# Top-128 search in a four-layer transformer kernel: the last count moves to VectorE, and TensorE builds two lists in PSUM for MAX8

## The reference, cut to what matters

```python
draft = einsum('bhqd,bhkd->bhqk', qr, kr) + causal_mask
_, draft_indices = top_k(draft, 128)             # num_remain = 128 for S = 512
mask = full(neg); mask[..., draft_indices] = 0.0 # then causal again
scores = einsum('bhqd,bhkd->bhqk', qr, kr) / sqrt(16) + mask
attn = softmax(scores); out = (attn @ v) @ Wo.T
```

## Time and profile before

| | |
|---|---|
| median of 3 runs | 2380.08 us (2378.83 to 2393.21) |
| profiled execution | 2377.4 us, its span 2375.6 us |
| mean granted TensorE clock | 0.834 |
| busy: PE / DVE / ACT / POOL | 1707.7 / 1615.9 / 1293.2 / 1017.7 us |

### The profile page before, as it was taken

The page is one execution under the profiler, slowest core; times in us unless marked ns, Lnnn a source line. Parts: engine busy times, 40 slices in busy tenths (PEclk is TensorE's granted clock), DMA queues, the critical chain, the costliest instruction groups (busy, mean ns, idle before and its releaser), DMA issues. The chain is left out here.

```text
span 2375.6 us, 25955 instructions
## 1 busy us (share of the span) xinstructions
PE 1707.7 (72%) x7274; PEld 1270.8 (53%) x7274; DVE 1615.9 (68%) x3711; ACT 1293.2 (54%) x3343; POOL 1017.7 (43%) x699
## 2 busy tenths in 40 slices
PE   5899998999898699998655433652545553387997
PEld 4777777777777578876422222331322222245885
DVE  3777777777776545656338898879779888822435
ACT  3555656556555332334167878776787778252221
POOL 3445545545444256552012344545434434632442
PEclk9999999999999799998556667775767776687998
DMA  4112111111111122212300000200000000001111
GB/s 151 32 43 91 41 50 56 67 57 54 60 41 58 54 80 104 82 53 99 58 7 7 7 8 1 27 7 1 8 7 7 7 7 1 1 0 45 48 45 49
DMA packets 33570, 96.40 MB, mean 41 GB/s; under 512 B 4048, under 2 KB 16720, under 8 KB 29264
## 3 DMA queue, kind: packets, MB, share of 16 engines
q1 hardware_dynamic: 33456, 95.20, 12.2%
HBM read 87.84 MB, written 7.34 MB: 40 GB/s over the span
## 5 line engine op out<-in xcount | busy, mean ns | idle before, releaser
L198 PE MATMUL PS<-XT,AR 128*128 128x512 f32 x2472 | 617.6, 405 | 26.0 <-POOL AR L805 12.3
L198 PE MATMUL PS<-AR 128*128 128x512 f32 (+2 forms) x2568 | 552.2, 370 | 100.4 <-issue 69.8
L198 PEld LDWEIGHTS PS<-AR 128*128 128x128 f32 x2568 | 449.5, 195 | 196.3 <-issue 91.5
L198 PEld LDWEIGHTS PS<-XT,AR 128*128 128x128 f32 x2472 | 469.4, 192 | 138.4 <-issue 16.8
L1244 POOL TENSOR_TENSOR AF<-AF 128x512 f32<-128x512 f32 (+3 forms) x64 | 148.5, 2320 | 487.7 <-DVE AF L1449 487.7
L1185 ACT ACTIVATE AF<-PS 128x512 f32<-128x512 f32 x160 | 94.0, 594 | 255.8 <-PE PS L1065 134.5
L1052 PE MATMUL PS<-AR,XT 48*128 48x128 f32 (+3 forms) x256 | 127.5, 498 | 142.4 <-DVE BF L1312 74.7
L1080 PE MATMUL PS<-AF,BF 128*128 128x512 f32 x320 | 191.6, 703 | 20.7 <-ACT AF L1185 20.5
L1100 PE MATMUL PS<-BF,AF 128*128 128x1 f32 x24 | 7.0, 362 | 264.3 <-DVE BF L1410 264.3
L559 POOL TENSOR_TENSOR AF<-AF 128x512 f32<-128x512 f32 (+1 forms) x64 | 107.6, 1681 | 167.8 <-DVE AF L690 167.8
L553 POOL TENSOR_TENSOR AF<-AF 128x512 f32<-128x512 f32 x80 | 103.3, 1292 | 168.2 <-ACT AF L345 168.2
(11 more groups left out here) (171 smaller groups left out, 3616.0 us busy)
## 6 DMA issues: line engine op xcount, KB each, us to landing
AF<-in_mean_w SPq DMA_DIRECT2D x48, 448.0 KB, 3.3
AF<-in_ffn_w SPq DMA_DIRECT2D x14, 1536.0 KB, 6.5
AF<-in_attn_w SPq DMA_DIRECT2D x9, 1536.0 KB, 6.4
AF<-in_attn_w SPq DMA_DIRECT2D x9, 1024.0 KB, 5.0
AF<-in_ffn_w SPq DMA_DIRECT2D x11, 769.0 KB, 4.4
XT<-rope_scratch SPq DMA_DIRECT2D x96, 64.0 KB, 2.7
rope_scratch<-BF SPq DMA_DIRECT2D x20, 256.0 KB, 2.3
AF<-in_x SPq DMA_DIRECT2D x8, 256.0 KB, 3.8
```

Of the source, the lines that this page charges most:

```text
L198: last = nc.tensor.matmul(dst, lhs(a, c), rhs(m, c), start=(first and k == 0), stop=(k == 3 * n - 1 and not more))
```

## The change

- The fourth count leaves ScalarE. VectorE does it with `mark`: 0 where a key is at or above the threshold, -1 where not, written as bf16 into one of three row buffers, and summed on the way.
- TensorE makes two lists for each head in PSUM (`lists`), by adding large numbers to recomputed scores: one where only keys below the threshold keep their score, one with negated scores where only keys above keep it. `pick` is now one MAX8 on each, straight from PSUM. The negated keys lie at partitions 64 to 111 (GpSimd, `negate`), so key and query tiles are loaded twice, at partitions 0 and 64.
- The aim is now 128, with up to 7 keys missing or too many. `cut` looks in both lists.
- The four score banks become one ring of slots for scores and lists (`ring_full`, `ring_free`).
- TensorE's loop begins with the 16 `lists` of x - 1. SyncE waits for `keys_read(x - 2)`.
- ScalarE's order is count 0, exp 0, count 1, exp 1, count 2, then the copies and exp 2 and 3. Update 2 on VectorE moves behind `evac` of q = 2.

```diff
-AIM = TOPK - (WINDOW + 1) // 2
+SIDE = (WINDOW + 1) // 2
+AIM = TOPK
...
+        def scored(x, h):
+            return 16 * x + 32 * before(x - 1) + h
+        def listed(x, h, side):
+            return 16 * min(x + 2, NB) + 32 * before(x) + 2 * h + side
+        def keys_read(x):
+            return (listed(x, 15, 1) if tile_of(x)[1] > 0 else scored(x, 15)) + 1
...
-                for x in (2 * n, 2 * n + 1):
-                    if x >= 2:
-                        sp.wait_ge(A1["scores"], 16 * (x - 1))
+                if x >= 2:
+                    sp.wait_ge(A1["ring_full"], keys_read(x - 2))
                 if n % QT == 0:
-                    if b > 0:
-                        sp.wait_ge(A1["scores"], QT * 32)
-                    for a, s in enumerate((0, 1, 0)):
-                        src = scr[b, 4, s].rearrange("(c h) t -> c h t", c=HD1)
-                        sp.dma_start(f32(kst[a * HD1:(a + 1) * HD1]), src).then_inc(A1["kst"], 16)
+                    for low in (0, 64):
+                        for a, s in enumerate((0, 1, 0)):
+                            src = scr[b, 4, s].rearrange("(c h) t -> c h t", c=HD1)
+                            sp.dma_start(f32(kst[low + a * HD1:low + (a + 1) * HD1, 4 * hf:4 * hf + 4]),
+                                         src[:, 4 * hf:4 * hf + 4]).then_inc(A1[f"kst{hf}"], 16)
+                for low in (0, 64):
                     for j in range(2):
                         for a, s in enumerate((0, 0, 1)):
...
+            def slot(k):
+                wait(pe, A1["ring_free"], k - 3)
+                return PS[:, k % 4]
...
+            def lists(x, h):
+                n, i, hf, W = tile_of(x)
+                q, k = qst[:, x % 2, h, :], kst[:, 4 * hf + h // G1, 0:W]
+                mark = above[:, h % 3, 0:W]
+                pe.wait_ge(A1["above"], 16 * before(x) + h + 1)
+                dst = slot(listed(x, h, 0))
+                nc.tensor.matmul(dst[:, 0:W], ident_b, causal_big[:, SEQ - W:SEQ], start=True, stop=False)
+                nc.tensor.matmul(dst[:, 0:W], negbig_b, mark, start=False, stop=False)
+                nc.tensor.matmul(dst[:, 0:W], q[0:48], k[0:48], start=False, stop=True).then_inc(A1["ring_full"], 1)
+                if h % 8 == 0:
+                    pe.wait_ge(A1["kneg"], 2 * (n // QT) + hf + 1)
+                dst = slot(listed(x, h, 1))
+                nc.tensor.matmul(dst[:, 0:W], big_b, mark, start=True, stop=False)
+                nc.tensor.matmul(dst[:, 0:W], q[64:112], k[64:112], start=False, stop=True).then_inc(A1["ring_full"], 1)
...
             for x in range(-1, NB + 2):
                 xp = x - 1
+                if 0 <= xp < NB and tile_of(xp)[1] > 0:
+                    for h in range(16):
+                        lists(xp, h)
                 if x + 1 < NB:
                     scores(x + 1, 0)
...
+            def mark(x, h):
+                n, i, hf, W = tile_of(x)
+                if h == 0:
+                    dve.wait_ge(A1["thr"], ROUNDS * (before(x) + 1))
+                v.tensor_scalar(above[:, h % 3, 0:W], S1[x % 2][:, h, 0:W], st["thr"][:, h:h + 1], -1.0,
+                                ALU.is_ge, ALU.add, accum_out=acc[:, 2, h:h + 1]).then_inc(A1["above"], 1)
+            def pick(x, h):
+                W = tile_of(x)[3]
+                for side in range(2):
+                    k = listed(x, h, side)
+                    dve.wait_ge(A1["ring_full"], k + 1)
+                    v.max(best[:, h, SIDE * side:SIDE * side + SIDE], PS[:, k % 4, 0:W]).then_inc(A1["ring_free"], 1)
...
             def cut(x):
+                step(v.tensor_scalar(missing, acc[:, 2], -1.0, float(TOPK - W), ALU.mult, ALU.add))
+                step(v.tensor_tensor(hit, at_tau.unsqueeze(1).to_broadcast([P, 16, 16]), rows, ALU.is_equal))
+                dve.wait_ge(A1["ring_free"], listed(x, 15, 1) + 1)
+                step(v.tensor_tensor(val, hit, best, ALU.mult))
+                step(v.tensor_reduce(below, val[:, :, 0:SIDE], AX.X, ALU.add))
+                step(v.tensor_reduce(over, val[:, :, SIDE:2 * SIDE], AX.X, ALU.add))
+                step(v.tensor_tensor(st["tau"][:, x % 2], below, over, ALU.subtract))
+                step(v.tensor_tensor(gap[:, :, 0:WINDOW], best[:, :, 0:WINDOW], best[:, :, 1:WINDOW + 1], ALU.is_gt))
+                step(v.tensor_tensor(hit, at_gap.unsqueeze(1).to_broadcast([P, 16, 16]), rows, ALU.is_equal))
+                step(v.tensor_tensor(val, hit, gap, ALU.mult))
+                v.tensor_reduce(flag_row, val.rearrange("p h s -> p (h s)"), AX.X, ALU.add).then_inc(A1["cut"], 1)
...
-                for pair in range(8):
+                if topk:
+                    mark(xp, 0)
+                    mark(xp, 1)
+                for h in range(16):
                     if topk:
-                        pick(xp, pair)
-                    if search and pair in (2, 5):
-                        update(x, (pair - 2) // 3)
-                    if done >= 0 and pair == 3:
+                        if h + 2 < 16:
+                            mark(xp, h + 2)
+                        pick(xp, h)
+                    if search and h in (6, 14):
+                        update(x, (h - 6) // 8)
+                    if done >= 0 and h == 7:
...
-                    if done >= 0 and pair == 7:
+                    if done >= 0 and h == 15:
                         dve.wait_ge(A1["yproj"], done + 1)
...
                     if x + 1 < NB:
                         evac(x + 1, q)
+                    if search and q == 2:
+                        update(x, 2)
...
+    at_tau = np.concatenate([np.where(j < SIDE - 1, j + 1, NONE), -j])
```

More of the change, by code:

```diff
@@ L957, in build_kernel @@
         A1 = names("a1", "raw_qkv", "raw_wo", "wq_hi", "wq_lo", "wk_hi", "wk_lo", "wv_hi", "wv_lo", "wo_hi", "wo_lo",
[L958 to L959 removed]
+                   "tables", "vproj", "v", "vz", "stored0", "stored1", "kst0", "kst1", "qst0", "qst1", "mask", "mask_r",
+                   "ring_full", "ring_free", "kneg", "above", "tiny", "stat", "nmax", "thr", "acc", "cut", "tau",
                    "flag_ps", "exp", "final", "rinv", "pnorm", "turned", "pt", "pv", "o_hi", "o_lo", "yproj", "yadd")
@@ L1046, in scores @@
                 if q == 0:
[L1047 to L1052, removed]
-                                     start=True, stop=False)
-                    nc.tensor.matmul(PS[:, h, W - P:W], ident_r, mask_r, start=False, stop=True)\
-                        .then_inc(A1["scores"], 1)
+                    pe.wait_ge(A1[f"kst{hf}"], 96 * (n // QT + 1))
+                    pe.wait_ge(A1[f"qst{x % 2}"], 16 * 12 * (x // 2 + 1))
+                for h in range(4 * q, 4 * q + 4):
+                    dst = slot(scored(x, h))
+                    nc.tensor.matmul(dst[:, 0:W], qst[0:48, x % 2, h, :], kst[0:48, 4 * hf + h // G1, 0:W],
+                                     start=True, stop=False)
+                    nc.tensor.matmul(dst[:, W - P:W], ident_r, mask_r, start=False, stop=True)\
+                        .then_inc(A1["ring_full"], 1)
+            def lists(x, h):
[12 more added lines that the diff above has]
+                nc.tensor.matmul(dst[:, 0:W], q[64:112], k[64:112], start=False, stop=True).then_inc(A1["ring_full"], 1)
             def values(x, q):
@@ L1188, in act_attn1 @@
                 xp = x - 1
-                search = x < NB and tile_of(x)[1] > 0
-                counted = 0
-                def last_round(heads=1):
-                    nonlocal counted
-                    if search:
-                        upto = min(counted + heads, 16)
-                        count(x, ROUNDS - 1, range(counted, upto))
-                        counted = upto
+                search, shown = x < NB and tile_of(x)[1] > 0, 0 <= xp < NB
                 if search:
@@ L1407, in cut @@
-                step(v.tensor_tensor(val, hit, best[:, :, 1:WINDOW + 1], ALU.mult))
-                step(v.tensor_reduce(after, val, AX.X, ALU.add))
-                step(v.tensor_tensor(after, after, st["tau"][:, x % 2], ALU.is_lt))
-                v.tensor_reduce(flag_row, after, AX.X, ALU.add).then_inc(A1["cut"], 1)
+                missing, below, over = st["square"], st["err"], st["scaled"]
+                rows = missing.unsqueeze(2).to_broadcast([P, 16, 16])
+                dve.wait_ge(A1["above"], 16 * (before(x) + 1))
@@ L1471, in dve_attn1 @@
                     cut(xp)
-                if search:
-                    update(x, 2)
                 if 0 <= xp < NB and xp % (2 * QT) == 0:
```

184 lines of the change are left out of this document (80 added, 104 removed).

## The result

| | before | after |
|---|---|---|
| median | 2381.39 us (2378.83 to 2393.21, 4 runs) | 7710.32 us (7695.58 to 7712.71, 4 runs) |
| profiled span | 2375.6 us | 7708.3 us |
| granted TensorE clock, mean | 0.834 | 0.613 |

The change makes the kernel 3.233 times slower (95% interval 3.222 to 3.245). The forecast was 2822 us, in a range from 2650 to 3150, so the time lies far outside it. The sign was right; the size was not, and by a mechanism that the forecast had excluded.

The account below looks back on a forecast made before the run. VectorE's queue was taken to set the pace of the searched steps. Picks -62, stall and tails +162, third update +11 and opening +3 gave +114; with a 328 us fallback, 2819 profiled or 2822 us median, range 2650 to 3150.

Parts of the forecast that it names:

- The marks and lists don't replace the picks: Rival for the new selection on VectorE and TensorE: it does not take over the old one; ruled out, given no chance.
- The branch back of the loop: Return branch per turn of the fallback loop in resolve: taken as 0.2 us, bounds 0 and 0.95.
- The signs that the prediction named: TensorE gaps of 9 to 10 us, yadd waiting 17 us, MAX8 pairs 1.83 us a head, one 256-turn step.
- One fallback at x = 9: In resolve, exactly one tile (256 keys) leaves the window and sorts all 16 heads: 328 us, bounds 260 and 520.
- Picks, gain 62 us: Selecting keys on VectorE and TensorE in the twelve searched steps falls from 370 to 309 us.
- The bound with all loads hidden: List matmuls on TensorE at 0.25 us each, VectorE setting the pace everywhere: 22 us more gain.
- at the end of a step TensorE ran at the high clock and the lists follow without a gap: Argument against lists on TensorE running at the low clock, which would make the picks 175 us more.
- The rival with a chance of 0.08: Lists on TensorE stay at 1.2 GHz: 3.0, 2.5 and 1.9 us a head, 2997 us in all; chance 0.08.
- The stall of the query loads and the tails, loss 162 us: Query loads exposed 9.7 us in twelve steps: even tails +8.4, odd +17.4, plus 7.5 in steps 7 and 8.
- Third update +11: VectorE's third update, moved behind evac of q = 2, costs +1 us a step: +11, bounds 0 and 29.
- opening loads +3: Tile 0's first loads grow by nine DMAs: 0 to 5.6 us, taken as 3.
- Sum without fallback: Whole kernel if no tile falls back: 2494 us; as a rival, chance 0.12.

Follow-up runs that it names:

- E1: The changed kernel with marks written by is_lt and second scalar 0, the lists' large identities swapped and cut's sign adapted: 2891.4 us (ratio 1.2136).
- E2: E1 with 0.34 instead of 0.36 in the first guess of the threshold, so no row of these inputs falls back: 2535.9 us (ratio 1.0658).
- E8: E4 plus six useless matmuls of 512 columns ahead of the wait for the first mark of every step: 2376.6 us (ratio 0.9970).
- E3: E2 with the lists' queries in a buffer of their own, so the scores' six query loads go out early as before: 2430.4 us (ratio 1.0199).
- E4: E3 with the projection issued behind the lists of head 10 instead of behind the next scores: 2388.9 us (ratio 1.0012).
- E9: E6 plus six useless matmuls ahead of the wait for the first mark of every step: 2358.0 us (ratio 0.9893).
- E6: E4 plus one useless matmul of 512 columns per head in the lists of 256 keys: 2360.6 us (ratio 0.9898).
- E5: The changed kernel with the mark split in two: one without accumulated output, one with it and second scalar -W into an unread row: 2971.8 us.
- E11: The changed kernel with only cut's reading of the sum mended (TOPK - 1 instead of TOPK - W), marks unchanged: 7714.8 us.
- E7: E6 plus 24 useless matmuls before the wait for a new batch's keys, scores waiting only for the low-partition keys: 2374.6 us (ratio 0.9952).

## Why the prediction was wrong, point by point

**The step that failed** is the rival that was dropped: "The marks and lists don't replace the picks can be ruled out from the diff." The diff shows what is issued, not what an operand means. The forecast took -1.0 and add as a step on each element, as the change's words and its `cut` do. No row of before shows the operation with a second scalar that matters, and `evac` reads the same either way. The branch back of the loop, of which no row showed a price, was bounded from both sides; this operation, of which no row showed the meaning, got neither a bound nor a chance. Its price could be worked out: eleven fallbacks more, 16 x 16 turns each. The forecast counted one fallback, and the runs showed twelve. From E1 to after they cost 7710.3 - 2891.4 = 4819 us, 438 each, since most are wider than 256 keys. The signs that the prediction named would not have caught it: it was to be wrong if the loop or the gaps were absent, and both are there.

What the forecast said of the change as it was meant is judged by E1 and E2.

**One fallback at x = 9: right.** E1 was 2891 us against 2822. Price 328 forecast, 355 measured. A turn was put at 1.2 us and took 1.34: the value load was 0.092 instead of 0.073, and idle time per turn 0.41 (1025.3 + 228.7 us over 3072, in after) where 0.29 was allowed. The page "Advanced Engine Details and Errata" of the Trainium skill (Control Flow Timing), by which the branch back is about 108 ns, pointed the wrong way for the sum: the loop's MAX8 alone was preceded by 0.33 us of idle time. That time holds a drain as well, so no run shows the branch by itself.

**Picks, gain 62 us: mostly not there.** Over the first eleven half-tiles E2's picks sum to 327.6 us, before's to 341.5: 14 us. (The forecast's 370 for before took one half-tile of each width; those with an even x took up to 2.2 us more, 39.0 at 512 keys.) By width, E2 against forecast: 384 keys 25.9 us (mean of four) against 25.3, right. 512 keys 34.5 against 31.0. 256 keys 30.2 against 20.9, four times 9 us. The prices of a head on TensorE at the high clock were good: 1.17 measured against 1.26 at 256 keys, 1.43 (1500.05 to 1501.48) against 1.52 at 384, 1.71 (1680.38 to 1682.09) against 1.79 at 512. So was the price at the low clock, in the rival: 1.88 against 1.9. The bound with all loads hidden, 5 x 0.25 = 1.25 us at 512 keys, was not reached. What failed is the argument that "at the end of a step TensorE ran at the high clock and the lists follow without a gap". In E2 five of the twelve lists have a gap of 1.0 to 1.6 us in front, and at 256 keys the clock falls even where the gap is filled (E8) or absent (x = 9 in E2); for x = 2 it was low before the lists began. The rival with a chance of 0.08 came true in the four half-tiles of 256 keys (mean clock 0.50 to 0.59 in their picks) and in part of three others (x = 6, 10 and 12, at 0.75 to 0.90).

**The stall of the query loads and the tails, loss 162 us: right.** Even tails were 15.9 to 18.0 us, 16.7 on average (forecast 17.1), odd ones 27.5 (26.1). All twelve sum to 265.2 us against 101.4 before, +164. The stall itself is 10.5 us (forecast 9.7). E3 and E4 show the cause, 106 + 41 = 147 us given back by two moves that change little else; the tails alone gave back 152.

**Third update +11, opening loads +3: too high.** From `tau` to the next first mark E2 needs 312.4 us over ten steps and before 310.3, so +2; the first mark of the search starts at 1249.23, where before the end of L1342 was at 1249.91, so nothing for the opening.

**Sum without fallback:** 2494 forecast, 2524 in E2's profiled execution, 2536 in the median. The missing 30 to 42 us come from three parts. E2's picks sum to 363 us where the forecast had 309, 54 more. The small parts cost some 12 less. And before's own picks were some 8 us longer than the 370 of the forecast, so that the gain was about 15 us instead of 62. Of the 54, an estimate lays 47 to the low clock. At 256 keys it is 37, from the stretches at 1.88 instead of 1.17 us a head. For x = 6 and 12 it is 10: they took 35.4 and 37.2 us in E2 and 31.1 in E1, at clock 1.00 and 0.98. The picks of x = 13 took 35.1 us at clock 1.00: their first MAX8 waited 4.95 us for the first list.

## What to carry to other kernels

A change that leans on an operand in a way that the old kernel never did has a rival with its own chance: that it computes something else, and what the kernel then does. Where there is a slow path for bad cases, price it for all cases, not for the one that you computed. And where TensorE sets the pace of a stretch at 1.2 GHz, look at what it runs there and at the idle microsecond in front. Useless matmuls in both were worth 1.3% here (E4 to E9); those inside the lists alone gave 28 of the 31 us (E6).

## What the runs showed of the hardware

- `tensor_scalar` with an accumulated output: op1 reduces, the second scalar is the start of the sum, and the elements written do not get it (E5 for the sum, E11 for the elements, 7714.8 us). Without one, op1 works on each element (E5, 2971.8 us).
- VectorE's two rates. Groups by form of after (busy us, mean ns), a copy and a mark at 512 keys, and the mark without accumulated output of E5:

```profile
L1441 DVE COPY BF<-BF 128x512 f32<-128x512 f32 x32 | 13.7, 427 | 3.1 <-DVE BF L1434 1.0
...
L1400 DVE TENSOR_SCALAR_CACHE_REDUCE SG<-BF 128x512 bf16<-128x512 f32 x32 | 23.1, 732 | 0.0
```

```profile
L1400 DVE TENSOR_SCALAR SG<-AF,BF 128x512 bf16<-128x512 f32 x32 | 15.1, 472 | 0.0
```

  The page "VectorE: DVE Perf Modes" of the Trainium skill (the perf-mode tier table) gives fp32 copies and `tensor_scalar` in SBUF the double rate. The rows agree for the copy (294 ns at 256 keys, 427 at 512) and for the plain mark (338 and 472), both 0.52 ns more per element, but not for the accumulated one: 732 ns, and 465 at 256 keys, 1.04 ns more per element. E5's two passes at 512 keys (472 + 739 ns) cost only 0.48 us a head more than the one.
- MAX8 reads PSUM as fast as SBUF: 433 against 428 ns at 256 keys, 691 against 695 at 512.
- TensorE's granted clock fell to 1.2 GHz while it was busy without a gap (lists of x = 3 in E2, from 1342.6 us on), and in lists of 512 keys it stayed there for over 40 us of unbroken work (x = 7 in E4). The page "TensorE: Matmul & The Clock Gate" of the Trainium skill (HAM oscillation) tells of falls that come of waits for DMA between bursts of matmuls. In the lists of 256 keys no such wait stands before the fall, and it comes with the gap ahead of them filled as well (E8), so the page's case is not this one. Why these lists lose the clock stays open.
- Behind a gap of 1.6 to 2.0 us the lists of x = 7 lost the clock in the profiles of E1, E3, E4 and E7 and kept it in those of after, E2 and E6, with the same matmuls in the lists. That this is what spreads E4's times over 30 us is likely (E8's lie within 10), but no single unprofiled execution shows it.
